# Attention: the rows of the maxima reach the queries by two transfers through a DRAM table instead of matmuls and a copy

## The reference

```python
q, k, v = (proj(Wq), proj(Wk), proj(Wv))       # 8 heads of 16, 2304 tokens an image
scores = jnp.einsum('bhqd,bhkd->bhqk', q, k) * scale
attn = jax.nn.softmax(scores, axis=-1)
out = jnp.einsum('bhqk,bhkd->bhqd', attn, v)
...
x = x + einsum('bsc,dc->bsd', out, Wo)         # back to (b, c, h, w)
```

## Time and profile before

| | |
|---|---|
| median of three runs | 2139.8 us (2138.97 to 2140.18) |
| profiled execution | 2140.26 us, span 2138.5 us |
| instructions | 35520 |
| warm-up of the maxima | 1011 to 1062 us |
| windows beside the sampling | 1062 to 1547 us |
| windows with the scores alone | 1601 to 2088 us |

### The profile page before, as it was taken

One profiled execution on the slowest core, in us unless ns is written; L12 is line 12 of the kernel. 1 busy time (PEld: TensorE's weight loads), 2 busy tenths in 40 slices (PEclk: granted clock), 3 DMA queues, 4 the chain that ended last, 5 costly groups with the idle time before them and its releaser, 6 DMA issues.

```text
span 2138.5 us, 35520 instructions
## 1 busy us (share of the span) xinstructions
PE 1690.1 (79%) x11841; PEld 898.8 (42%) x11841; DVE 1749.9 (82%) x4137; ACT 1183.1 (55%) x3185; POOL 1074.6 (50%) x1232
## 2 busy tenths in 40 slices
PE   4222123249988899966899999999999999999998
PEld 2111112125554476654455555555444444444433
DVE  5888889878999799955888888888888888888871
ACT  3222222210000177764488888888677777777777
POOL 3777777726666377773777777775030000000000
PEclk8555555559999899998799999999999999999999
DMA  8777677720001166672534334432011011111101
GB/s 274 210 210 211 209 207 210 210 59 1 1 1 37 51 186 177 179 245 64 143 104 112 112 95 112 111 103 60 15 25 30 12 23 29 23 23 25 19 2 45
DMA packets 90856, 212.15 MB, mean 99 GB/s; under 512 B 18513, under 2 KB 43825, under 8 KB 90545
## 3 DMA queue, kind: packets, MB, share of 16 engines
q0 software_dynamic: 51840, 169.91, 26.9%
q1 hardware_dynamic: 38832, 39.97, 8.3%
HBM read 175.21 MB, written 13.37 MB: 88 GB/s over the span
## 4 chain that ended last, share of the span: by engine, by line
PE 45%; ACT 4%; DVE 2%; issue 2%; POOL 1%; DMA 0%; SPq 0%; ACTq 0%; POOLq 0%
PE ps L1859 14%; PE ps L1821 14%; PE ps L1837 11%; ACT l_e L1567 2%; PE ps L1917 2%; DVE l_mx L1691 1%; PE ps L1907 1%; PE ps L1844 1%; ACT corner L1538 1%; PE ps L1871 1%; PE ps L1877 0%; POOL corner L1425 0%; PE ps L1898 0%; POOL l_part L1434 0%; PE ps L1884 0%
## 5 line engine op out<-in xcount | busy, mean ns | idle before, releaser
L1691 DVE TENSOR_REDUCE l_mx<-ps 128x1 f32<-128x384 f32 x1728 | 835.8, 548 | 125.3 <-PE ps L1837 125.0
L1567 ACT ACTIVATE l_e<-ps 128x384 f32<-128x384 f32 x1728 | 726.8, 512 | 213.1 <-PE ps L1821 210.7
L1837 PE MATMUL ps<-l_ka,l_qs 96*128 96x384 bf16 x1728 | 573.3, 334 | 15.0 <-DMA l_qs<-l_part 8.8
L1821 PE MATMUL ps<-l_qs,l_ks 99*128 99x384 bf16 x1728 | 564.2, 331 | 4.8 <-ACT l_part L1594 1.6
L830 DVE SCALAR_TENSOR_TENSOR m_prod<-ps,c_b,pad 128x384 f32<-128x384 f32 x588 | 323.6, 607 | 39.8 <-PE ps L1035 38.6
L1859 PE MATMUL ps<-l_e,l_v_s 128*32 128x384 f32 x3456 | 333.4, 492 | 2.0 <-ACT l_e L1567 1.0
L549 PE MATMUL ps<-c_ident,l_samp 128*128 128x128 f32 x324 | 77.6, 424 | 312.4 <-DVE x_map L417 294.7
L1821 PEld LDWEIGHTS ps<-l_qs,l_ks 99*128 99x128 bf16 x1728 | 165.8, 97 | 360.5 <-ACT l_e L1567 190.3
L1464 POOL CAST l_nsp<-l_nm 128x3 bf16<-128x3 f32 x96 | 18.3, 191 | 522.2 <-DVE l_nm L1696 491.2
L259 POOL DMA_INDIRECT corner<-table,idx x216 | 204.8, 948 | 92.8 <-issue 64.6
L1035 PE MATMUL ps<-red,c_w 32*128 32x384 f32 x1176 | 193.1, 570 | 40.0 <-DVE m_prod L830 35.4
(11 more groups left out here) (212 smaller groups left out, 1886.1 us busy)
## 6 DMA issues: line engine op xcount, KB each, us to landing
corner<-table,idx POOLq DMA_INDIRECT x540, 3.7
l_ka<-l_part SPq DMA_DIRECT2D x96, 72.0 KB
l_ks<-l_part SPq DMA_DIRECT2D x96, 72.0 KB
table<-l_tok SPq DMA_DIRECT2D x8, 640.0 KB, 7.3
table<-red SPq DMA_DIRECT2D x8, 640.0 KB, 6.2
l_qs<-l_part SPq DMA_DIRECT2D x90, 48.0 KB
l_qs<-l_part SPq DMA_DIRECT2D x96, 24.0 KB
out<-x_map SPq DMA_DIRECT2D x12, 192.0 KB, 1.9
```

The lines of the kernel that those rows point to most:

```text
L1567: nc.scalar.activation(e[:, w % 2, i, :], ps[:, st_bank(at), 0:QC], ACT.Exp).then_inc(s["st_free"], 1)
L1691: nc.vector.tensor_reduce(mx[:, ga % MAX_SLOTS, u // NQC, u % NQC:u % NQC + 1], ps[:, ab_bank(at), 0:CH], AX.X, ALU.max) \
L1821: nc.tensor.matmul(ps[:, bank, 0:QC], ks[:, head % 2, kt * 128:(kt + 1) * 128], qs[:, gb % 3, j * QC:(j + 1) * QC], start=True, stop=True) \
L1837: nc.tensor.matmul(ps[:, bank, 0:CH], qs[0:KROWS, ga // CT % 3, q0:q0 + 128], ka[:, head % 2, k0:k0 + CH], start=True, stop=True).then_inc ...
```

## The change

The three matmuls, ACT's copy and their entries in the score ring go, with the bf16 identity and its cast on POOL. In their place SP writes `nsp` of a chunk to a table in DRAM (`maxima`, four slots of 3 x 128 x 3 bf16), waits until that has landed (semaphore `away`), and reads it back as three rows of 384 into rows 96 to 98 of `qs`. PE's first score of a batch waits for the four loads of that batch (`rows0` and `rows1` in turn) in place of ACT's copy. POOL's split of a chunk waits for the loads of the whole batch that had its slot before. PE's wait for the constants stands behind the warm-up.

```diff
-ROWS_WARM = (29, 47, 65, 83)
-ROWS_AT = (2, 4, 6, 8)
...
+        row = [s["rows0"], s["rows1"]]
+        away = nc.dram_tensor("maxima", [MAX_SLOTS, 3, 128, MROWS], BF16).ap()
...
+        def row_total(gb):
+            return 16 * CT * (gb // 2 + 1)
...
+                def rows(gb):
+                    for ga in range(gb * CT, (gb + 1) * CT):
+                        sp.wait_ge(s["nsplit"], ga + 1)
+                        at = ga % CT * QC
+                        sp.dma_start(away[ga % MAX_SLOTS].rearrange("i p m -> p i m"), nsp[:, ga % MAX_SLOTS, :, :]).then_inc(s["away"], 16)
+                        sp.wait_ge(s["away"], 16 * (ga + 1))
+                        sp.dma_start(qs[KROWS:KROWS + MROWS, gb % 3, at:at + QC],
+                                     away[ga % MAX_SLOTS].rearrange("i p m -> m (i p)"),
+                                     allow_slow_non_contiguous=True).then_inc(row[gb % 2], 16)
...
+                rows(0)
                 for gb in range(BATCHES):
...
+                    if gb + 1 < BATCHES:
+                        if gb >= 2:
+                            sp.wait_ge(s["st_full"], no.st["score", (gb - 1) * WPB - 1, 2 * CT - 1] + 1)
+                        rows(gb + 1)
...
-                chain.link(nc.gpsimd.tensor_copy(identb[:, :], g["ident"][:, :]))
...
                     if ga >= MAX_SLOTS:
-                        pool.wait_ge(s["st_full"], no.st["rows", ga - MAX_SLOTS] + 1)
+                        gb = (ga - MAX_SLOTS) // CT
+                        pool.wait_ge(row[gb % 2], row_total(gb))
...
-                def take_rows(ga):
-                    at = no.st["rows", ga]
-                    act.wait_ge(s["st_full"], at + 1)
-                    nc.scalar.copy(qs[KROWS:KROWS + MROWS, ga // CT % 3, ga % CT * QC:(ga % CT + 1) * QC],
-                                   ps[KROWS:KROWS + MROWS, st_bank(at), 0:QC]).then_inc(s["st_free"], 1)
...
                     if i == 0 and at == 0:
-                        pe.wait_ge(s["st_free"], no.st["rows", gb * CT + CT - 1] + 1)
+                        pe.wait_ge(row[gb % 2], row_total(gb))
...
-                def rows(ga):
-                    pe.wait_ge(s["nsplit"], ga + 1)
-                    bank = enter_st(no.st["rows", ga])
-                    for i in range(3):
-                        last = nc.tensor.matmul(ps[KROWS:KROWS + MROWS, bank, i * 128:(i + 1) * 128],
-                                                nsp[:, ga % MAX_SLOTS, i, :], identb[:, :], start=True, stop=True,
-                                                tile_position=(0, KROWS))
-                    last.then_inc(s["st_full"], 1)
```

More of the change, by code:

```diff
@@ L1195 @@
 ATT_SEMS = GN_SEMS + ("const ones proj part1 part2 part3 less split kmax0 kmax1 key0 key1 query_first query0 query1 query2 "
-                      "v_slot st_full st_free ab_full ab_free av_mm negmax nsplit o_sb ochain z_in "
+                      "away rows0 rows1 v_slot st_full st_free ab_full ab_free av_mm negmax nsplit o_sb ochain z_in "
                       "saved pchain scaled mixed")
@@ L1208, in __init__ @@
                 self.st["value", n] = len(self.st)
-            if n in ROWS_WARM:
-                self.st["rows", ROWS_WARM.index(n)] = len(self.st)
             if n % 9 == 8:
@@ L1220, in __init__ @@
                 if j == BURST:
-                    if at in ROWS_AT and gb < BATCHES - 1:
-                        self.st["rows", (gb + 1) * CT + ROWS_AT.index(at)] = len(self.st)
                     if at == TURN_AT and gb:
@@ L1292, in attention_layer @@
         nsp = sb("nsp", [128, MAX_SLOTS, 3, MROWS], BF16)
-        identb = sb("identb", [128, 128], BF16)
         o_s = sb("o_s", [128, QC])
@@ L1611, in _ @@
                         take_value(n)
-                    if n in ROWS_WARM:
-                        take_rows(ROWS_WARM.index(n))
                     if n % 9 < 8 and n % 2:
@@ L1623, in _ @@
                     for i in range(2 * CT):
-                        if i == BURST and at in ROWS_AT and gb < BATCHES - 1:
-                            take_rows((gb + 1) * CT + ROWS_AT.index(at))
                         exp(w, i)
@@ L1931, in _ @@
                         value(n)
-                    if n in ROWS_WARM:
-                        if n == ROWS_WARM[0]:
-                            pe.wait_ge(s["const"], 1)
-                            pe.wait_ge(s["ones"], 1)
-                        rows(ROWS_WARM.index(n))
                     if n % 9 == 8:
                         beat(n // 9)
+                pe.wait_ge(s["const"], 1)
+                pe.wait_ge(s["ones"], 1)
                 for w in range(WINDOWS):
@@ L1946, in _ @@
                         if j == BURST:
-                            if at in ROWS_AT and gb < BATCHES - 1:
-                                rows((gb + 1) * CT + ROWS_AT.index(at))
                             if at == TURN_AT and gb:
```

## The result

The changed kernel takes 2760.3 us (median of 4 runs, 2754.9 to 2767.7) against 2139.4 before: a ratio of 1.290 [1.288, 1.293]. The forecast was 2127, and 2245 was the end of the range. The step that failed is the price of the small packets, 9 ns each on one of three engines. A load of 3 x 384 two-byte pieces takes 13.5 us from its issue to its landing, not 5.7, and the next load doesn't overlap it, where the forecast had counted only the last one. Four of them take 54 us, more than the 40 us in which PE does a batch, so the loads and not PE set the pace. That is the rival "the three engines are full", which had a chance of 0.13.

The account below looks back on a forecast made before the run. PE was taken to set the pace from the first score on. From 2140.3 us, less 20.7 gain, plus 10 of stalls gave 2129.6; counting 2 of batch 0's 5 us gave 2126.6, forecast 2127, range 2117 to 2245.

Parts of the forecast that it names:

- the three engines are full: Rival on the row loads: above 26 ns a packet they outlast a 40 us batch and set the pace; chance 0.13.
- The gain: PE's score stream: dropping three matmuls and a ring entry per chunk saves 12.4 us early and 8.3 late, 20.7 in all.
- The deadline: Each batch's start: last chunk's split to first score leaves 7.7 us late, 9.4 early, for store and load.
- Three engines: The load of rows into qs: one engine per outermost row, 384 packets one after another on each.
- The small packets: The row load's two-byte packets: 9 ns each, 3.5 us a load, for a latency of 7.7 us with the store.
- Above 26 ns: Threshold for the full-engines rival: beyond this packet price, 4 x 384 packets take longer than a batch of 40 us.
- Only a read latency that isn't overlapped would do that: Argument on the row loads: nothing else would give the full-engines case, such as 50 ns a packet, some 2900 us.
- 72 packets: Row load spread over all 16 engines: 72 packets each at 9 ns, 0.7 us, for a latency of 5.6 us.
- the stalls eat the gain: Rival at batch starts: 12 to 14 ns a packet, stalls of 24 to 39 us, 2135 to 2144 us; chance 0.10.
- the statement on POOL: POOL's split of the next batch's chunk 4 waits for the same loads as PE, so late only when PE is.
- SP is done with the rows by then: SP's queue: next queries behind the rows lose nothing, since rows finish by the batch's end or the batch hasn't begun.
- the wait for the loads becomes the bound of every batch: Rival at batch starts: two-byte packets cost 14 to 24 ns like 512-byte ones, 2191 to near 2300 us; chance 0.27.

Follow-up runs that it names:

- the kernel without rows: Against the changed kernel: neither matmuls nor transfers bring the rows, which are set to zero once, exp scaled by 0.01; 2118.9 us, 0.990 of the kernel before.
- b_three: Changed kernel with each load of three rows issued as three loads of one row; 2613.0 us, 1.222 of the kernel before.
- h_probe: Kernel before plus 21 transfers behind its last store, each waited for, list run twice; the changed kernel's load of 3 x 384 took 14.8 and 12.7 us.
- j_loads: Changed kernel without its stores: loads issued at once after each split, from a table of zeros; 2585.4 us, 1.209 of the kernel before.
- c_zero: Changed kernel, store kept, but the load takes three contiguous 768-byte rows from a table of zeros; 2150.3 us, 1.005 of the kernel before.
- e_turned: Changed kernel with the turn made by the store, in 1152 pieces of 2 bytes, and a contiguous load; 2789.5 us, 1.304 of the kernel before.

## Why the prediction was wrong, step by step

**The gain** (20.7 us of 2140) was right: 20.0 by the kernel without rows. The burst before a fourth score takes 1.86 us in late windows of the changed kernel, as foretold. Two scores on its two sides, in a window that had the three matmuls before:
```profile
2283.46 0.34 PE L1824 MATMUL ps<-l_qs,l_ks 99*128 99x384 bf16 x1
...
2285.32 0.34 PE L1824 MATMUL ps<-l_qs,l_ks 99*128 99x384 bf16 x1
```
**The deadline** was the right question, and its slack the right size: in the kernel without rows a late batch starts 7.7 us after its last split. Batch 16 needs 24.9 and stalls 17.2. **Three engines** for this load follow from the rule of the Trainium skill, page "DMA: Bandwidth & Descriptors", section "Why a DMA increments its semaphore by 16 and not by 1". The trace agrees: the semaphore that counts a load is raised four times for it, once 0.4 us after the issue and three times as it lands, where each of b_three's one-row loads, with 384 outermost, raises it 16 times. But it doesn't decide the time, as b_three shows.

**The small packets** are the step that failed, in two ways. The size: I took 9 ns from seven semaphore packets and 24 from 512-byte ones as an upper end. In those terms the load costs 13.5 / 384 = 35 ns for each packet of an engine: 0.9 us to the first packet, 6.5 to 8 for the packets, and 5 more until it counts as landed. A packet's length in the trace is what its own record spans, and rows that show only that bound nothing from above. I called 24 ns an upper end because 512 bytes are more than 2, and that was a guess about a mechanism, not a row. The store's 1.9 us was for long pieces; this one took 4.5 with nothing in flight, since its 384 pieces of 6 bytes lie side by side.

The nature: I added occupation to one chunk's latency only, and let the store of a chunk meet an empty queue. The store's landing has this row over 1062 to 2700 us, median 11.0 us:
```profile
maxima<-l_nsp SPq DMA_DIRECT2D x94, 2.2 KB, 11.0
```
A chunk comes every 10 us and its load holds the path for 13.5, so the store waits behind the load of the chunk before. **"Above 26 ns"** was the right threshold for the rival of the full engines (4 x 384 packets against 40 us), and 35 ns is past it. By its own arithmetic 35 ns gives 54 us a batch. Measured are 58.5 to 69, because each chunk's store stands between the loads. What spoke against that rival was only the 9 ns. "Only a read latency that isn't overlapped would do that" was wrong: the same 1152 cells are read in 2.7 us when they go to 128 rows (h_probe), so it is the writing into three rows.

Two sums of the prediction don't come out. With 72 packets the latency is 4.2 + 0.7 = 4.9 us, not 5.6. And "the stalls eat the gain" adds 24 to 39 us to 2119.6, which is 2144 to 2159 and not 2135 to 2144, so all but its lower end was a loss that can be told. Neither touches the forecast or what failed.

**The sum again, in measured terms**, from first score to last score: the changed kernel's 1646 us against 1062 hold 554 us of longer gaps before the first scores of batches 1 to 23 (564.2 in place of 10.1). The late start of batch 0 adds 43 (1105.0 in place of 1061.7; I had counted 2). The remaining 30 us stand inside the batches: some 50 lost, less the 20 of gain. Without its gap a late batch takes 41.2 us and an early one 49.3; without rows they take 39.1 and 46.9. These 2.1 to 2.4 us a batch go with the clock. The stages of the stall before batch 16, of its first 4 us and of the rest (columns as above, granted clock ahead of the DMA share):
```profile
2246.00:2263.30 17.30, 0.24 (x2) 0.00 (x0) 1.55 (x4) 0.81 (x3) 0.00 (x0) 0.60 0.38 33
2263.30:2267.40 4.10, 4.00 (x22) 1.25 (x22) 1.67 (x3) 1.47 (x3) 0.77 (x4) 0.59 0.36 45
2267.40:2304.00 36.60, 36.45 (x271) 14.43 (x268) 32.25 (x71) 26.68 (x68) 2.34 (x12) 1.00 0.19 1
```
After 17 us in which PE does nothing, the trace grants it 0.50, 1.2 GHz, for 3.2 us more, until 2266.6, and then 1.00, 2.4 GHz; the 0.59 of the middle row is the mean over both. In batches 1 to 23 the stretches at 0.50 after a stall's end add up to 105 us. Work at half the clock loses half its time, so that makes 52 us by estimate, against the 50 that are lost. No experiment took that apart, but the first 4 us behind such a stall are granted 0.50 in b_three and 0.55 in j_loads too. Of the gaps, j_loads has 366 us, so the loads alone make two thirds of them, and the rest comes with the stores, by difference.

**What stands behind the moved waits**: the statement on POOL held (its split is late in the same 23 places). That on SP failed. "SP is done with the rows by then" is false for batch 11, whose rows stand behind the wait for the second image's split. It cost 13 us in c_zero, and in the changed kernel the gap there is 44.7 us where its neighbours have 11.2 and 23.2. I had priced only the lateness of what the rows hold up, not that the rows themselves stand behind this wait, four in a row.

**The rivals**: that the wait for the loads becomes the bound of every batch (2191 to 2300) had the sign and the place, but a price of at most 24 ns. "Engines full" had the mechanism. I gave it 0.13 for want of a row. A range should have reached it, as nothing in the trace excluded it. The Trainium skill, same page, section "Specifications", says that below 512 bytes a read-modify-write is made. The runs show no jump there: 1152 pieces of 32 to 256 bytes to or from 128 rows took 2.2 to 2.4 us, and of 512 bytes 3.1 to 4.0. The jump lies between 2 and 4 bytes in writes to three rows (14.4 and 7.2 us), and at neighbouring cells in DRAM.

## What to carry to other kernels

Ask of every transfer how many pieces it writes, how long each is and how many rows or neighbouring cells they share; 1152 two-byte pieces into three rows of SBUF cost 13.5 us when three engines bring them and 11.6 when 16 do, and it is occupation, so it is multiplied by every transfer between two deadlines. Durations of packets don't bound a landing; if no row of the trace shows such a transfer, keep the case "its path is full" inside the range. Where a small tile must be turned, turn it on an engine first (here 32 x 32 on DVE) and let the transfers carry whole runs.

## What the runs showed of the hardware

- Packet records can end long before the transfer counts as landed: a store of 384 six-byte pieces passes in 0.3 us and lands 3.2 to 4.1 us after the last when nothing else is in flight; 1152 two-byte ones over 16 engines pass in 1.3 us (e_turned) and 2.0 (b_three) and land about 11 and 8.3 us later (medians).
- Two-byte writes into three rows of SBUF are special: 4-byte pieces in the same number take half the time (7 against 14 us), and 8 to 64 bytes (5.8 to 7.0) little less than 4. Into 128 rows 2-byte pieces take 3 us.
- In DRAM, small writes to neighbouring cells are slow (15 us for 1152 of 2 bytes side by side, 2.7 to 2.9 at 512 bytes distance); reading such cells costs nothing extra (2.7 us to 128 rows, 2.6 at 512 bytes distance).
- An issue of SP that takes 0.25 to 0.4 us elsewhere lengthened to 3.44 us (a store) and 6.18 us (a load of j_loads) while earlier loads of small pieces were under way, so even a transfer that waits for nothing can hold back what is behind it on SP.
